# Diagonal matrices and loads of x in other slices, and another order of the closing stage, in a wavelet attention and SwiGLU kernel

## The reference, cut to what matters

```python
# x: [2, 4096, 512] f32
low = x; highs = []; lens = []
for _ in range(2):                       # two levels of a filter bank
    lens.append(low.shape[1])
    l = dwconv(low, h_filter)[:, ::2]    # 4 taps for each channel, every second row
    h = dwconv(low, g_filter)[:, ::2]
    highs.append(h); low = l
q = elu(low) + 1                         # linear attention, 16 heads of 32 channels, k = q, v = low
low = (q @ (k^T v)) / (q . sum(k) + 1e-6)
for h, L in zip(reversed(highs), reversed(lens)):
    low = dwconv(repeat(low, 2), h_synth) + dwconv(repeat(h, 2), g_synth)
mixed = layer_norm(x + low) * gamma + beta
x = _layernorm(x + mixed)
# feed-forward: weights are int32, 1536 x 512, times 1/127
h = silu(x @ wg.T) * (x @ wu.T)
out = _layernorm(x + h @ wd.T)
```

## Time and profile before

| | |
|---|---|
| median of 3 runs | 1210.11 us (1209.3 to 1210.5) |
| the profiled execution's own time | 1209.61 us |
| its span, first to last instruction | 1207.8 us |
| mean granted TensorE clock | 0.994 |
| PE, DVE, ACT, POOL busy | 1173.7 us (97%), 973.1 us (81%), 672.6 us (56%), 303.1 us (25%) |

### The profile page before, as it was taken

How to read it: one execution, slowest core, us unless ns; L and a number is a source line. 1 busy time by engine, 2 the same in 40 slices (tenths; PEclk the granted TensorE clock), 3 DMA queues, 4 the chain that set the end, 5 groups by cost and what they waited for, 6 DMA issues and landing times.

```text
span 1207.8 us, 19489 instructions
## 1 busy us (share of the span) xinstructions
PE 1173.7 (97%) x6456; PEld 604.4 (50%) x6456; DVE 973.1 (81%) x1951; ACT 672.6 (56%) x1403; POOL 303.1 (25%) x730
## 2 busy tenths in 40 slices
PE   6888999999999999999999999999999999999997
PEld 5567644445445544445445444444445444454443
DVE  7797999998999989997997779867997689845331
ACT  6954744677346854576346644666346644565342
POOL 0014322152314313152213412142304313131101
PEclk9998999999999999999999999999999999999999
DMA  7886520222212310222102310211111310110000
GB/s 263 271 201 142 184 61 19 106 97 89 71 44 79 128 40 18 98 83 74 36 27 97 98 35 18 105 62 53 35 58 64 106 35 11 42 55 1 3 34 35
DMA packets 52301, 92.96 MB, mean 77 GB/s; under 512 B 9072, under 2 KB 28784, under 8 KB 51312
## 3 DMA queue, kind: packets, MB, share of 16 engines
q1 hardware_dynamic: 50480, 87.10, 21.9%
q0 software_dynamic: 1728, 4.72, 2.2%
HBM read 67.09 MB, written 25.19 MB: 76 GB/s over the span
## 4 chain that ended last, share of the span: by engine, by line
PE 81%; DVE 6%; ACT 5%; issue 4%; POOL 3%; DMA 1%; SPq 0%; POOLq 0%; ACTq 0%; DVEq 0%
PE ps_up L679 12%; PE ps_up L680 12%; PE ps_gate L679 12%; PE ps_gate L680 12%; PE ps_down L698 12%; PE ps_down L697 12%; PE ps_x L622 2%; PE ps_y L640 2%; DVE l L1286 1%; PE ps_x L601 1%; POOL rs L1216 1%; PE ps_down L864 1%; DVE h L1286 1%; ACT x_hi L1136 1%; DVE hid L1286 1%
## 5 line engine op out<-in xcount | busy, mean ns | idle before, releaser
L697 PE MATMUL ps_down<-w,hid 128*128 128x512 f16 x768 | 291.4, 379 | 1.2 <-DVE hid L1672 1.0
L698 PE MATMUL ps_down<-w,hid 128*128 128x512 f16 x768 | 291.3, 379 | 0.0
L679 PE MATMUL ps_up<-x_hi,w 128*128 128x512 f16 x760 | 288.4, 379 | 0.9 <-DVE h_f L1685 0.9
L679 PE MATMUL ps_gate<-x_hi,w 128*128 128x512 f16 x760 | 288.4, 379 | 0.5 <-ACT h_f L1160 0.5
L680 PE MATMUL ps_gate<-x_lo,w 128*128 128x512 f16 x760 | 288.3, 379 | 0.0
L680 PE MATMUL ps_up<-x_lo,w 128*128 128x512 f16 x760 | 288.2, 379 | 0.0
L1160 ACT ACTIVATE h_f<-ps_gate 128x512 f32<-128x512 f32 x192 | 113.9, 593 | 205.6 <-PE ps_gate L680 204.6
L1685 DVE SCALAR_TENSOR_TENSOR h_f<-ps_up,h_f 128x512 f32<-128x512 f32 x192 | 130.9, 685 | 110.1 <-PE ps_up L680 97.7
L1152 ACT ACTIVATE hid<-h_f 128x512 f16<-128x512 f32 x192 | 119.7, 623 | 42.0 <-DVE h_f L1685 42.0
L1672 DVE TENSOR_TENSOR hid<-h_f,hid 128x512 f16<-128x512 f32 x192 | 130.9, 682 | 1.9 <-ACT hid L1152 1.0
L679 PEld LDWEIGHTS ps_up<-x_hi,w 128*128 128x128 f16 x760 | 74.2, 98 | 91.5 <-DVE h_f L1685 1.8
(11 more groups left out here) (260 smaller groups left out, 1688.0 us busy)
## 6 DMA issues: line engine op xcount, KB each, us to landing
xt<-x_tok SPq DMA_DIRECT2D x64, 256.0 KB, 2.7
out<-x SPq DMA_DIRECT2D x64, 256.0 KB, 2.0
xb<-x_chan SPq DMA_DIRECT2D x7, 2060.0 KB, 7.7
xa<-x_chan SPq DMA_DIRECT2D x20, 515.0 KB, 5.0
w<-weights POOLq DMA_DIRECT2D x12, 384.0 KB, 9.9
att<-den SPq DMA_DIRECT2D x32, 129.5 KB, 2.7
xa<-x_phase SPq DMA_DIRECT2D x8, 515.0 KB, 6.4
q_in<-q_scratch SPq DMA_DIRECT2D x7, 518.0 KB, 4.5
```

The lines of the kernel that those rows point to most:

```text
L679: pe.matmul(ps_gu[k % 2][g][:, :], w, x1_hi[:, b, c, :], start=(c == 0), stop=False)
L697: pe.matmul(ps_d[t % 2][:, :], h_hi[:, k, t * P:(t + 1) * P], w, start=(k == 0), stop=False)
L698: mm = pe.matmul(ps_d[t % 2][:, :], h_lo[:, k, t * P:(t + 1) * P], w, start=False, stop=(k == NH - 1))
```

## The change

- `DIAGS` gives the diagonals by (first, count): 4 at the head of slice 0, 5 inside slice 0 behind `pro_band_firsts`, 3 each in slices 1, 2 and 3, and 10 in slice 4, each of these at the place of before.
- Both loads of `xb` are issued in slice 3, behind the other loads of that slice.
- `CLOSE_PE`: `attend` 2 and 3 ahead of `h_conv` (2,0) instead of behind it.
- `CLOSE_ACT`: `h_conv` (3,0) ahead of `h1` 1.
- `CLOSE_DVE`: `attend` 3 and `h1` 0 ahead of `lowT` (1,0); `lowS` (1,1) from ahead of tile 0's `norm2a` to behind `sT` (1,1); `lowT` (0,1) ahead of `norm3` 0. The four `xbeta`, which stood in a loop ahead of the list, are its first four entries.
- `CLOSE_POOL`: `norm2` 1 ahead of `norm1` 2, and `norm1q` 3 ahead of `norm2` 2.

```diff
--- before.py
+++ after.py
@@ -134,31 +134,31 @@
 
 
 NPRO = PER_BATCH + 1
+DIAGS = ((0, 4), (4, 5), (9, 3), (12, 3), (15, 3), (18, 10))
 H0W, H1W = DSUB * P // 2, M1 - DSUB * P // 2
 SYN = (T0, T12, T0 + 3, T01, T23, S0, S12, S0 + 3, S01, S23)
 LOW_E, LOW_O = ((T0, 0), (T12, 1), (T0 + 3, 2)), ((T01, 0), (T23, 1))
 ATT_E, ATT_O = ((S0, 0), (S12, 1), (S0 + 3, 2)), ((S01, 0), (S23, 1))
-CLOSE_PE = [("h_conv", (2, 0)), ("attend", 2), ("attend", 3), ("h_conv", (3, 0)), ("attend", 0), ("attend", 1),
+CLOSE_PE = [("attend", 2), ("attend", 3), ("h_conv", (2, 0)), ("h_conv", (3, 0)), ("attend", 0), ("attend", 1),
             ("low", (2, 0)), ("low", (3, 0)), ("s", (2, 0)), ("s", (3, 0)), ("h_conv", (2, 1)), ("h_conv", (3, 1)),
             ("norm1", 0), ("low", (2, 1)), ("norm1", 1), ("low", (3, 1)), ("norm1", 2), ("s", (2, 1)), ("norm1", 3),
             ("norm3", 0), ("s", (3, 1)), ("norm3", 1), ("norm3", 2), ("gu", (0, 0, 0)), ("gu", (0, 1, 0)),
             ("gu", (1, 0, 0)), ("norm3", 3), ("gu", (1, 1, 0))]
-CLOSE_ACT = [("h1", 0), ("low", (0, 0)), ("low", (1, 0)), ("h_conv", (2, 0)), ("low", (0, 1)),
-             ("h1", 1), ("h_conv", (3, 0)), ("low", (1, 1)), ("exp4", 1),
-             ("low", (2, 0)), ("low", (3, 0)), ("h_conv", (2, 1)), ("h_conv", (3, 1)), ("norm1", 0),
-             ("norm1q", 0), ("low", (2, 1)), ("norm1", 1), ("norm1q", 1), ("normq", 0), ("norm1", 2),
-             ("low", (3, 1)), ("normx", 0), ("norm1q", 2), ("normq", 1), ("norm1", 3), ("norm3", 0), ("norm1q", 3),
-             ("normx", 1), ("normq", 2), ("norm3", 1), ("normx", 2), ("normq", 3), ("norm3", 2), ("normx", 3),
-             ("norm3", 3)]
-CLOSE_DVE = [("lowT", (0, 0)), ("attend", 2), ("lowT", (1, 0)), ("attend", 3), ("h1", 0), ("attend", 0),
-             ("sT", (1, 0)), ("attend", 1), ("sT", (0, 0)), ("lowS", (1, 0)), ("lowS", (0, 0)), ("s_add", (2, 0)),
-             ("sS", (0, 0)), ("sS", (1, 0)), ("s_add", (3, 0)), ("lowT", (1, 1)), ("h1", 1), ("lowS", (1, 1)),
-             ("norm2a", 0), ("norm2b", 0), ("sT", (0, 1)), ("norm2a", 1), ("norm2b", 1), ("sT", (1, 1)),
-             ("norm2a", 2), ("norm2b", 2), ("norm3", 0), ("lowT", (0, 1)), ("norm2a", 3), ("norm2b", 3),
-             ("lowS", (0, 1)), ("norm3", 1), ("sS", (0, 1)), ("norm3", 2), ("sS", (1, 1)), ("norm3", 3),
-             ("s_add", (2, 1)), ("s_add", (3, 1))]
-CLOSE_POOL = [("norm1", 0), ("norm1q", 0), ("norm1", 1), ("norm2", 0), ("norm1q", 1), ("normq", 0), ("norm1", 2),
-              ("norm2", 1), ("norm1q", 2), ("normq", 1), ("norm1", 3), ("norm2", 2), ("norm1q", 3), ("normq", 2),
+CLOSE_ACT = [("h1", 0), ("low", (0, 0)), ("low", (1, 0)), ("h_conv", (2, 0)), ("low", (0, 1)), ("h_conv", (3, 0)),
+             ("h1", 1), ("low", (1, 1)), ("exp4", 1), ("low", (2, 0)), ("low", (3, 0)), ("h_conv", (2, 1)),
+             ("h_conv", (3, 1)), ("norm1", 0), ("norm1q", 0), ("low", (2, 1)), ("norm1", 1), ("norm1q", 1),
+             ("normq", 0), ("norm1", 2), ("low", (3, 1)), ("normx", 0), ("norm1q", 2), ("normq", 1), ("norm1", 3),
+             ("norm3", 0), ("norm1q", 3), ("normx", 1), ("normq", 2), ("norm3", 1), ("normx", 2), ("normq", 3),
+             ("norm3", 2), ("normx", 3), ("norm3", 3)]
+CLOSE_DVE = [("xbeta", 0), ("xbeta", 1), ("xbeta", 2), ("xbeta", 3), ("lowT", (0, 0)), ("attend", 2), ("attend", 3),
+             ("h1", 0), ("lowT", (1, 0)), ("attend", 0), ("sT", (1, 0)), ("attend", 1), ("sT", (0, 0)),
+             ("lowS", (1, 0)), ("lowS", (0, 0)), ("s_add", (2, 0)), ("sS", (0, 0)), ("sS", (1, 0)), ("s_add", (3, 0)),
+             ("lowT", (1, 1)), ("h1", 1), ("norm2a", 0), ("norm2b", 0), ("sT", (0, 1)), ("norm2a", 1), ("norm2b", 1),
+             ("sT", (1, 1)), ("lowS", (1, 1)), ("norm2a", 2), ("norm2b", 2), ("lowT", (0, 1)), ("norm3", 0),
+             ("norm2a", 3), ("norm2b", 3), ("lowS", (0, 1)), ("norm3", 1), ("sS", (0, 1)), ("norm3", 2),
+             ("sS", (1, 1)), ("norm3", 3), ("s_add", (2, 1)), ("s_add", (3, 1))]
+CLOSE_POOL = [("norm1", 0), ("norm1q", 0), ("norm1", 1), ("norm2", 0), ("norm1q", 1), ("normq", 0), ("norm2", 1),
+              ("norm1", 2), ("norm1q", 2), ("normq", 1), ("norm1", 3), ("norm1q", 3), ("norm2", 2), ("normq", 2),
               ("norm2", 3), ("normq", 3)]
 
 
@@ -515,8 +515,9 @@
                     pro_q_store(a - 1)
                     hold(sp, pro_conv1, 2 * a + 2)
                     load_pro(a + 1, 2)
-                if a in (1, 2):
-                    sp.dma_start(xb[:, a + 1, :], x_chan[:, 0, a + 1, :]).then_inc(ld_xb0, 16)
+                if a == PER_BATCH - 1:
+                    for c in (2, 3):
+                        sp.dma_start(xb[:, c, :], x_chan[:, 0, c, :]).then_inc(ld_xb0, 16)
                 if a == PER_BATCH:
                     for t in range(4):
                         load_xt(0, t)
@@ -1099,6 +1100,7 @@
                                              scale=phase_coef(c, h, n)).then_inc(diag_g_ready, 1)
             for a in range(NPRO):
                 if a == 0:
+                    pro_diags(*DIAGS[0])
                     pro_l1(a, 0)
                     pro_l1(a, 1)
                 else:
@@ -1106,6 +1108,9 @@
                 pro_out1_copy(a, 3)
                 pro_band_firsts(a, 0)
                 pro_band_firsts(a, 1)
+                if a == 0:
+                    act.wait_ge(coef_ready, 6)
+                    pro_diags(*DIAGS[1])
                 pro_out1_copy(a, 2)
                 if a > 0:
                     pro_turn_copy(a - 1, 0)
@@ -1113,10 +1118,8 @@
                 if a > 0:
                     pro_turn_copy(a - 1, 2)
                     pro_turn_copy(a - 1, 3)
-                if a == 1:
-                    act.wait_ge(coef_ready, 6)
-                if 1 <= a <= 3:
-                    pro_diags(10 * (a - 1), 10)
+                if a > 0:
+                    pro_diags(*DIAGS[a + 1])
                 pro_out2_copy(a, 3)
                 pro_out2_copy(a, 2)
                 if a < PER_BATCH:
@@ -1657,9 +1660,8 @@
             dve.wait_ge(sums_zero, 3)
             closing = {"h1": pro_h1, "attend": pro_attend, "lowT": pro_low_h2, "lowS": pro_low_att, "sT": pro_s_high,
                        "sS": pro_s_low, "s_add": pro_s_add, "norm2a": lambda t: norm2_centre(0, t),
-                       "norm2b": lambda t: norm2_scale(0, t), "norm3": lambda t: norm3(0, 0, t)}
-            for t in range(DSUB):
-                xbeta(0, 0, t)
+                       "norm2b": lambda t: norm2_scale(0, t), "norm3": lambda t: norm3(0, 0, t),
+                       "xbeta": lambda t: xbeta(0, 0, t)}
             for name, n in CLOSE_DVE:
                 closing[name](n)
             after(taps_done[0])
```

## The result

| | before | changed |
|---|---|---|
| median of 22 runs | 1209.39 us | 1211.54 us |
| lowest and highest | 1207.42, 1210.97 | 1207.64, 1214.97 |
| profiled execution: time, span, mean clock | 1209.61, 1207.8, 0.994 | 1207.64, 1205.8, 0.996 |

The ratio, estimated over all runs, is 1.0014, with a 95% interval of 1.0007 to 1.0020 (the two medians alone would give 1.0018): the changed kernel is slower by 1.7 us (0.0014 x 1209.4), inside the 0.2% within which I had put it, and by more than the 0.65 us of the sum. The changed kernel's executions also spread more widely, 7.3 us against 3.6.

The account below looks back on a forecast made before the run. TensorE bounds the untouched long stage; ahead of it no engine does, only a relay of waits. Slices +0.35 and GpSimd's order +0.3 give +0.65: 1210.3, or 1210.7 us as the median, range 1207.6 to 1212.8.

Parts of the forecast that it names:

- the sum: Whole change: slices +0.35 us and the later `norm2` 2 on GpSimd +0.3, together +0.65.
- The bound: TensorE-bound long stage untouched; relays ahead of it; closing work before GpSimd's `norm1` 0 has about 2.7 us of slack.
- The diagonals in the slices: Slices 0 to 4: delay of +1.2 us, then +1.0, then +0.3 to +0.4; slice 4's ten nearly fit; +0.35 carried.
- The loads of x: Slices: -0.1 to -0.2 us in slice 2, +0.2 at the last store, unseen by VectorE; bounds nothing and 1.5.
- rival D: Slice 4: last h store queues fully behind the two loads, up to 1.5 us, giving 1211.7; chance 0.06.
- GpSimd's start: Closing stage: it hangs on the last `att` DMA and so on the denominator, +0.35 us.
- GpSimd's order: Closing stage: `norm2` 2 behind `norm1q` 3 comes 0.65 us later, about 0.3 gets through; bounds 0 and 0.8.
- rival B: Slice 3 and `s` (2,1): low clock goes away; about 1209, 1208.2 or, both gone, 1206.7; chance 0.16.
- Rival C: Low clock lasts to `s` (3,1) in the closing stage, 1215, or newly hits slice 1 or 2, 1212.3; chance 0.12.
- my own sign: TensorE's clock: the forecast is wrong if the 0.50 clock stretches sit elsewhere.
- The ports: Closing stage: VectorE's `lowS` (1,1) beside GpSimd's powers would add up to 0.4 us by the rule, if nothing hid it.
- the likeliest case: Whole kernel: the forecast taken alone, 1209.9 to 1211.8 us; chance 0.58.

Follow-up runs that it names:

- e3_close: The kernel before with only the four reordered lists of the closing stage; 1209.49 us, ratio 0.9996.
- e1_diags: The kernel before with only the diagonals moved; 1210.82 us, ratio 1.0007.
- g2_loads_back_warm: The changed kernel with extra unused matmuls in TensorE's waits and the two `xb` loads back in slices 1 and 2; 1209.03 us, ratio 0.9999.
- f3_before_warm: The kernel before with extra unused matmuls, ten ahead of the transposes of slices 1 to 4 and twenty-four ahead of `s` (2,1); 1208.73 us, ratio 0.9995.
- f1_behind_store: The changed kernel with the two `xb` loads issued right behind the last h store instead of ahead of it; 1212.39 us, ratio 1.0014.
- g1_diags_out: The changed kernel with slice 0's five diagonals made in slice 1 instead, eight there; 1209.78 us, ratio 1.0004.
- e0_after: The changed kernel as it is, timed again against the kernel before; 1212.41 us, ratio 1.0016.
- e2_loads: The kernel before with only the two `xb` loads moved to slice 3; 1209.94 us, ratio 0.9999.
- f4_after_warm: The changed kernel with extra unused matmuls in TensorE's waits, in slices 1 to 4 and ahead of `s` (2,1); 1210.63 us, ratio 1.0007.
- f2_pads_late: The kernel before with the four zero-pad stores issued behind the reloads of xt instead of ahead of the weight loads; 1206.94 us, ratio 0.9977.
- g4_after_pads_late: The changed kernel with the zero-pad stores issued late; 1206.08 us, ratio 0.9979.

## Why the prediction was right, and where it was not

- *The bound*: right. The bulk is unchanged, and the closing lists up to `norm1` 0 hide behind GpSimd: e3_close is at 0.9996. The half microsecond that TensorE was to gain is not shown: in the changed kernel's profile it was 0.48 us sooner at tile 0, with a reciprocal 0.25 sooner, but in e3_close it was 0.43 later (96.52 against 96.09), with a reciprocal 0.35 later.
- *The diagonals in the slices*: right in size up to slice 2 in the first profile. Forecast were +1.2, +1.0 and +0.3 to +0.4 at the copies of slices 0 to 2; measured +1.27, +1.07 and +0.22. Slice 4's ten fitted into its idle time too: without a low stretch the copy came at 69.69 in e1_diags, against 69.68. That +0.35 is all that arrives at the reciprocal is not shown: at full clock it was 1.1 us late without the moved loads (g2_loads_back_warm against f3_before_warm, whose extra matmuls change the slices as well). What the step left out is that the new wait of TensorE in slice 0, 1.2 us by the plan and 1.17 in the first profile, is itself a place where the clock can fall. It did in two of the profiles with these diagonals (e1_diags, f1_behind_store), for another 1.0 to 1.5 us on the sixteen matmuls behind it, and in no profile without them. In both the wait was 2.05 us or more; where it was 1.0 to 1.4 the sixteen took their 1.95. It is not the whole of the lower clock either, which g1_diags_out has without these five.
- *The loads of x*: the term mis-sized. I had -0.1 to -0.2 in slice 2 and +0.2 hidden at the last store, with 1.5 as the bound, and rival D for that bound with a chance of 0.06. The last store took 6.1 to 7.4 us in all profiles with the loads ahead of it, 1.5 to 2.9 more. That is rival D's mechanism. VectorE's slack did not take it in: the reciprocal came 1.6 us late in e0_after and 2.1 in e2_loads. Slice 2 got back up to 0.9. What the store costs in the end is not shown: e2_loads had the slow store and is at 0.9999, f1_behind_store had it cured and is at 1.0014, and g2_loads_back_warm and f4_after_warm start their bulk 0.04 us apart. Whether the parts cost more together than apart is open too (e1_diags, e2_loads and e3_close add up to 0.2 us, the whole to 1.9, each of the four within about 1.1, so the gap is within noise).
- *GpSimd's start*: the mechanism was another. I had the weights hang on the last `att` transfer. They begin when it lands, at 77.6 in e0_after and 78.3 before, although e0_after's reciprocal was later. Some two to four of GpSimd's 15 to 17 us without an issue are the zero-pad stores, which SP issues right behind the `att` transfers and so behind the reciprocal: in e0_after and e2_loads the second issue of weights came 27.4 and 27.6 us behind the first `att` issue, before 27.9 (though 28.7 in e1_diags and 28.9 in e3_close, for no reason that I can show). The slow stretch moves with the pads: e0_after issued them from 74.77, before from 72.89, and the three windows of 2 us from 80 had 35, 40 and 134 GB/s there, 51, 157 and 211 before. With the pads late the second issue came 22.8 to 25.3 us behind the first `att` issue, and the later reciprocal had the sooner issue. That is the likely way by which the reciprocal's delay got through all the same; f2_pads_late and g4_after_pads_late bear it out.
- *GpSimd's order*: +0.3 forecast, nothing found. From the first `norm3` on TensorE to the bulk it is 12.06 us before (113.48 to 125.54), 12.05 in the changed kernel, in e0_after and in e3_close. ScalarE got to `normq` 2 1.05 us later against the first `norm3` (3.73 us behind it and not 2.68; forecast was 0.65). But GpSimd's three operations behind that took 0.31, 0.55 and 0.19 us instead of 0.74, 0.55 and 0.35, the shift was ready 0.5 us later, and that much slack `normx` 2 had: it started 5.95 us behind the first `norm3`, against 5.90.
- *The clock*: rival B came true in the one profile of the change only for slice 3 (at full clock, 1.44 us sooner); in slice 4 the thirty-two matmuls then took 5.04 us instead of 3.68. By my own sign, low stretches elsewhere, that counted against me. Rival C did not come in the place where I had put it. I had argued against large differences between executions from three runs within 1.2 us; 22 lay within 3.6, and the change's within 7.3. Rival B's prices also had a slip in them: 2.8 us off 1210.7 is 1207.9 and not 1208.2. By the rule of the Trainium skill (TensorE: Matmul & The Clock Gate, What's actually happening) the gate runs free of the kernel, and the trace agrees: the slices of before, e3_close and f2_pads_late are the same code, and in the windows from 16 to 28, 28 to 40 and 40 to 53 us the profiles had 1.00, 1.00 and 0.89, then 0.86, 0.91 and 0.95, then 1.00, 1.00 and 0.87.
- *The ports*: the Trainium skill's rule (SBUF — State Buffer, Who interferes with whom) would have lengthened GpSimd's powers beside `lowS` (1,1). The power at 108.35 stood wholly beside it and took 0.55 us, so no cost was seen. The five taps are short, 0.28 us each; beside instructions of 0.75 us powers took 0.94.

So the forecast was right in its bound and its range, and the time fell where the likeliest case had it, 1211.54 within 1209.9 to 1211.8. Of that some is luck: the loss is 1.7 us and not 0.65, 0.3 of the 0.65 stands for a cost that did not come, and the signs for the end of the prologue missed in the first profile (GpSimd's first norm operation, forecast between 100.2 and 100.7, came at 99.31, and the bulk, forecast near 126.2, at 123.61; in e0_after they came at 101.13 and 126.1). The steps that failed are the price of the loads at the last store, the way from the reciprocal to the weights, and a clock taken to be the same on average. What the runs show in their place is a reciprocal some 1.6 us late that gets through to the bulk (1.3 us of it at full clock in both kernels), and a lower clock in more executions. How the late reciprocal divides between the diagonals and the loads stays open.

## What to carry to other kernels

Ask of each moved transfer which store or load on the relay stands behind it in the queue, and price that one, not the moved one; a store of 512 KB went from 4.5 us to between 6.1 and 7.4. Then time the move alone: here it cost nothing that could be measured. Look for transfers of a few bytes ahead of large ones: four stores of 24 KB in all, moved out of the way, were worth more than all the reordering here. And where waits of TensorE are moved about for free, compare the granted clocks of all executions, before and after, and not those of one profile: the lower clock went with a good part of the loss here. A few matmuls of no use in the waits took the low stretches away, but too many of them stood in the way.

## What the runs showed of the hardware

- GpSimd issued seven weight loads of 384 KB at 0.56 us each, then issued nothing until the DMA engines had run out of work (a share of 0.02 from 96 to 98 us before, with the next issue at 97.44). That took 14.8 to 17.4 us, and 12.5 to 13.3 with the pads late. All else in its stream waited behind it.
- The weight loads, with their cast, moved 201 to 219 GB/s at a DMA share of 1.05 to 1.12. Zero pads of 4 and 8 KB issued ahead of them took 4 to 7 us each to land (3.9, 5.5, 6.3 and 4.6 before), and beside them the rate was 51 GB/s for 2 us and 157 for the next two.
- The same wait in the same code left TensorE's clock alone in one execution and was followed by half of it in another. Ahead of slice 1's transposes, before and then in e3_close, which is the same code up to there:

```profile
23.56 0.44 PE L782 MATMUL ps_x<-ident,q_in 128*128 128x128 f32 x2 [2.31 <-DVE q_in L1526]
...
25.46 1.95 PE L763 MATMUL ps_down<-hid,kvt_mem 128*64 128x256 f32 x16
```

```profile
23.24 0.44 PE L782 MATMUL ps_x<-ident,q_in 128*128 128x128 f32 x2 [2.33 <-DVE q_in L1526]
...
25.95 2.76 PE L763 MATMUL ps_down<-hid,kvt_mem 128*64 128x256 f32 x16
```

- Over the executions of the changed kernel the time went with the mean granted clock, from 1207.6 us at 0.996 to 1215.0 at 0.991. With extra matmuls in the waits the clock was 1.00 throughout the prologue in the profiles of all four kernels that had them in the slices' waits.
